# Turning and dividing the attention outputs of 8-wide heads after the last maximum, in a 12-stage kernel

## The chip, the cores and the metric

One Trainium2 chip, one core of it. The time is the device time of one execution in microseconds (us), and the figure that counts is the median of the runs. PE is the matrix engine (PEld are its weight loads, which run beside its matmuls), DVE the vector engine, ACT the scalar engine, POOL the third elementwise engine, SP the queue that issues the loads and stores. PSUM is the accumulator memory, eight banks of 128 x 512 float32; SBUF is the working memory.

## What is computed

Twelve residual stages over 2048 tokens of 128 numbers. Two of them, stage 4 and stage 10, are attention with 16 heads that are 8 wide, and only they are touched:

```
q, k, v = heads(x @ Wq + bq), heads(x @ Wk + bk), heads(x @ Wv + bv)   # 16 heads, 8 wide
# stage 10 alone: rotary turn of q and k, a bias by distance, causal mask
att = softmax(q @ k^T * scale, axis=-1)
y = att @ v                                    # 2048 x 8 for each head
x = x + y.reshape(2048, 128) @ Wo + bo
```

Stage 4 attends to all 2048 keys, stage 10 only to keys at or before the query. The other ten stages are feed-forward layers, one local attention, one linear attention and so on.

## The kernel before

Both stages are the class `Attn8`. The work is cut into 16 rounds; a round is four heads and 512 queries. A round is cut into steps of 128 keys: 16 steps a round in stage 4 (256 in all), and 4, 8, 12 or 16 in stage 10 (160 in all), where the later 512 queries see more keys. Scores are made transposed, keys on the partitions and queries along the row.

Softmax needs the maximum of each query over all keys before its scores are exponentiated. PE makes a second set of scores for this (`max`, line 1894), queries on the partitions, in whichever of banks 5, 6 and 7 is next in a ring, and DVE reduces each 128 x 512 block to one number for each query (line 2107; in stage 10 a block that touches the diagonal goes through a custom add-and-max, line 2104). These maxima run ahead of the rounds that need them. When a round's maxima are complete, DVE closes them (`close`, line 2113), POOL splits them in two parts (lines 2169, 2171), and PE turns them into a row (`max_rows`, lines 1906, 1909) that the scores take in.

The order of everything is written out by `lay_plan` as one list, and each engine runs through its own part of that list in order. In a step the list holds: up to two maxima ahead of the scores, the scores of heads 0 and 1 and of heads 2 and 3 (line 1925, banks 0 and 1, then 2 and 3), `step` (ACT takes the exponential, line 2024), further maxima, a due `max_rows`, a due `finish`, the products with v of the step before (`values`, line 1942, bank 4), further maxima. Followed through for the kernel before, the list puts 4 maxima in each of steps 0 to 235 of stage 4 and the last 2 in step 236, so 19 steps follow without any. In stage 10 the last 2 maxima stand in step 137, and 22 steps follow. In stage 10 the steps near the diagonal ("near" steps) also have a bias, which goes through ACT (2014, 2017, 2029), POOL (2177) and DVE (2120).

A round ends when its last `values` is done. ACT copies bank 4, outputs transposed with the sum of the exponentials as a ninth row of each head, to `self.OT` (line 2033, two buffers). In the second step of the next round the list has `finish`: PE turns the four 128 x 128 pieces into the next bank of the ring (line 1951), DVE takes the reciprocal of the sums (line 2127) and multiplies (line 2129) into `self.AO`, which is `g.XN`. The finish of round n stands at step 16n + 17 of stage 4, for n up to 14; the finishes of stage 10 stand at steps 5, 13, 25, 41, 57, 69, 77, 81, 85, 93, 105, 121, 137, 149 and 157. The one of round 15 follows the last step. After it PE turns all of `AO` (line 1956) and projects it (line 1963).

`self.P` holds q and k in three bfloat16 parts; SP stores them to DRAM at the start of the stage, and they are not read afterwards. `self.RC` (4 x 512 float32) is a workspace of the same opening part.

Of the kernel before, what the change touches and what calls it, by code (L numbers as in the profile page):

```python
# [8 lines left out]
ACT = mybir.ActivationFunctionType  # L9
# [1463 lines left out]
class Attn8(Stage):  # L1473
# [10 lines left out]
    def allocate(self, g):  # L1484
        ar = g.ar
        self.causal = causal = self.k == 10
        self.pre = "L3a_" if causal else "L1a_"
        self.names = ("wq", "wk", "wv", "wo", "wqr", "wkr") if causal else ("wq", "wk", "wv", "wo")
        self.scale = 8.0 ** -0.5 if causal else 0.25
        self.W = ar.f32(6 if causal else 4, 128)  # L1490
        self.bqk = ar.f32(4 if causal else 2)
        self.bvb = ar.f32(2, 128)
        if causal:
            g.wr.at = 0
            self.ROT = g.wr.f32(2, 2048)
        self.slots = slots = 2 if causal else 4
        self.RC = ar.f32(4, 512)
        self.P = ar.bf16(2, 3, 2048)
        self.rows = {name: ar.bf16(slots, 2048) for name in ("KA", "KC", "QA", "QB", "QC")}
        self.VF = ar.f32(NT * 144 + 24)  # L1500
        self.VV = self.VF[:, 0:NT * 144].rearrange("p (a b c) -> p a b c", a=NT, b=16)
        self.AO = g.XN
        self.MX = ar.f32(2, 4, 4, 4)
        self.MT = ar.f32(2, 4, 4)
        self.MN = ar.bf16(2, 4, 128)
        self.OT = ar.f32(2, 512)
        self.RD = ar.f32(2, 4, 4)
        self.junk = ar.bf16(2, 512)
        self.warm = ar.f32(2)
        if causal:  # L1510
            self.BF, self.BN = g.near_bias
            self.NB = ar.f32(2, 2, 256)
            self.F2 = ar.f32(2, 512)
        else:
            self.KEPT = ar.f32(6, 512)
            self.NQ = ar.bf16(512)
        self.PB = ar.f32(4, 1024)
        assert not causal or ar.at <= 41500 - 9216
        self.rounds = [(gr, qc) for gr in range(4) for qc in ((0, 1, 2, 3) if (gr % 2 == 0) == causal else (3, 2, 1, 0))]
        self.last_kt = [4 * qc + 3 if causal else NT - 1 for gr, qc in self.rounds]  # L1520
        self.parts = [(c, j) for c in range(4) for j in (1, 0)] if causal else [
            (0, 1), (3, 0), (1, 1), (2, 1), (3, 1), (2, 0), (0, 0), (1, 0)]
        self.lay_plan()
# [77 lines left out]
    def lay_plan(self):  # L1601
# [24 lines left out]
        finish_due = []  # L1626
        self.left[0], self.left[1] = (("xt", 2),), (("xt", 3),)
        for x in range(len(self.parts) + 2):
            if x < len(self.parts):
                c, j = self.parts[x]  # L1630
                b = 2 * (x % 2) if causal else x % 4
# [37 lines left out]
        for i, (n, kt) in enumerate(steps):  # L1669
            goal = self.target(p + area[i])  # L1670
            pairs = [self.next_max(half, goal, 3) for half in (1, 0)]
            if causal:
                order = [x[y] + (2 * x[y][1] + z,) for y in range(3) for x in pairs if y < len(x) for z in range(2)]
                slots = [[x for y, x in enumerate(order) if 4 * y // max(4, len(order)) == z] for z in range(4)]
            else:
                order = [x[y] for y in range(3) for x in pairs if y < len(x)]
                slots = [order[0:1], [], order[1:], []]
            for u in range(2):
                for x in slots[u]:
                    self.plan_max(*x)  # L1680
                self.plan.append(("score", i, n, kt, u, self.hold(2 * u, ("exp", i, 1) if u else ("left", i)) + self.hold(2 * u + 1)))
            self.plan.append(("step", i, n, kt))
            for x in slots[2]:
                self.plan_max(*x)
            if self.rows_due:
                self.plan_rows_max(self.rows_due.pop(0))
            if finish_due:
                self.plan_finish(finish_due.pop(0))
            elif side:
                self.plan_rows(side.pop(0))  # L1690
            if i >= 1:
                pn, pk = steps[i - 1]
                if pk // 4 not in self.rows_made:
                    self.plan_rows(side.pop(0))
                self.plan.append(("values", i - 1, pn, pk))
                if pk == last_kt[pn]:
                    finish_due.append(pn)
            for x in slots[3]:
                self.plan_max(*x)
            self.plan_closed()  # L1700
            p += area[i]
        self.plan.append(("values", len(steps) - 1, *steps[-1]))
        for n in finish_due + [15]:
            self.plan_finish(n)


    def wait_left(self, e, s, old):

# [140 lines left out]
    def tensor(self, e, s):  # L1849
        g, k = self.g, self.k  # L1850
        KA, KC, QA, QB, QC = (self.rows[name] for name in ("KA", "KC", "QA", "QB", "QC"))
        turn_tensor(e, s, g, k, g.XN, "xn")
        seen = set()
        for what, *x in self.plan:
            if what == "compact":
                y, c, j, b, old, old_turned = x
# [10 lines left out]
            if what == "rows":  # L1867
                i, b, old = x
                self.wait_left(e, s, old)
                for y in range(4):  # L1870
                    o = 512 * i + 128 * y
                    t = e.matmul(g.bank[b][:, 128 * y:128 * y + 128], g.XT[:, o:o + 128], self.W[:, 2, :],
                                 start=True, stop=True, skip_group_check=True)
                t.then_inc(*s.up("row", k, i))
            if what == "max":
                n, st, kc, heads = x
                (gr, qc), w = self.rounds[n], min(512, self.keys_of(n, st) - 512 * kc)
                q, i = gr % self.slots, 4 * self.rounds[n][1] + st
# [18 lines left out]
            if what == "max_rows":  # L1897
                n, b, old = x
                gr, qc = self.rounds[n]
                self.wait_left(e, s, old)  # L1900
                name = self.score_rows_in(gr, qc, False)
# [6 lines left out]
                for i in range(4):  # L1908
                    t = e.matmul(g.bank[b][:, 128 * i:128 * i + 128], self.MN[:, n % 2, i, :], g.identb[:, :], start=False,
                                 stop=True, skip_group_check=True)  # L1910
                t.then_inc(*s.up("m_turned", k, n))
            if what == "score":
                i, n, kt, u, old = x
# [5 lines left out]
                name = self.score_rows_in(gr, kt // 4, True)  # L1919
# [3 lines left out]
                for y, (K, Q) in enumerate(((KA, QA), (KA, QB), (KC, QC))):  # L1923
                    for h in (2 * u, 2 * u + 1):
                        t = e.matmul(g.bank[h][:, lo:512], K[32 * h:32 * h + 32, q, 128 * kt:128 * kt + 128],  # L1925
                                     Q[32 * h:32 * h + 32, q, queries], start=y == 0, stop=y == 2, skip_group_check=True)
                t.then_inc(*s.up("scored", k, i, u))
            if what == "values":
                i, n, kt = x
# [10 lines left out]
                for h in range(4):  # L1940
                    o = 144 * kt + 9 * (4 * gr + h)
                    t = e.matmul(g.bank[self.O][32 * h:32 * h + 32, lo:512], self.VF[:, o:o + 32],  # L1942
                                 self.PB[:, y + h // 2, 512 * (h % 2) + lo:512 * (h % 2) + 512], start=kt == 0,
                                 stop=kt == self.last_kt[n], skip_group_check=True)
                t.then_inc(*s.up("valued", k, i))
            if what == "finish":
                n, b, old = x
                self.wait_left(e, s, old)
                e.wait_ge(*s.at("ot", k, n))
                for i in range(4):  # L1950
                    t = e.transpose(g.bank[b][:, 128 * i:128 * i + 128], self.OT[:, n % 2, 128 * i:128 * i + 128], g.ident)  # L1951
                t.then_inc(*s.up("o_turned", k, n))
        for c in range(4):
            e.wait_ge(*(s.at("xt", k, c - 2, "out") if c > 1 else s.at("finished", k, 15)))
            for i in range(4):
                t = e.transpose(g.bank[c % 2][:, 128 * i:128 * i + 128], self.AO[:, 4 * c + i, :], g.ident)
            t.then_inc(*s.up("turned", k, c, "out"))
        for c in range(4):
# [3 lines left out]
            for i in range(4):  # L1962
                t = e.matmul(g.bank[2 + c % 2][:, 128 * i:128 * i + 128], g.XT[:, 512 * c + 128 * i:512 * c + 128 * i + 128],
                             self.W[:, 3, :], start=True, stop=True, skip_group_check=True)
            t.then_inc(*s.up("projected_out", k, c))

    def scalar(self, e, s):
        g, k = self.g, self.k
        turn_scalar(e, s, g, k)
        in_kept = {}  # L1970
        for what, *x in self.plan:
            if what == "first":
                y, c, j, b = x
# [8 lines left out]
            if what == "second":  # L1982
                y, c, j = x
# [4 lines left out]
            if what == "max":  # L1988
                n, st, kc, heads = x
# [8 lines left out]
            if what == "max_rows":  # L1998
                n, b, _ = x
# [4 lines left out]
            if what == "step":  # L2004
                i, n, kt = x
                near, lo = self.near_cols(n, kt), self.low(n, kt)
                for u in range(2):
                    src = g.ps[:, 1024 * u:1024 * u + 1024].rearrange("p (a b) -> p a b", a=2)
                    dst = self.PB[:, (2 * kt + u) % 4, :].rearrange("p (a b) -> p a b", a=2)
                    if u == 0 and near:  # L2010
# [3 lines left out]
                        t = e.activation(nb, src[:, :, first:end], ACT.Copy)  # L2014
# [14 lines left out]
                    e.activation(dst[:, :, first:end], nb, ACT.Exp, scale=self.scale).then_inc(*s.up("exp", k, i, 0))  # L2029
            if what == "values" and x[2] == self.last_kt[x[1]]:  # L2030
                i, n, kt = x
                e.wait_ge(*s.at("valued", k, i))
                e.activation(self.OT[:, n % 2, :], g.bank[self.O], ACT.Copy).then_inc(*s.up("ot", k, n))
        for c in range(4):
            e.wait_ge(*s.at("turned", k, c, "out"))
            e.activation(g.XT[:, chunk(c)], g.bank[c % 2], ACT.Copy).then_inc(*s.up("xt", k, c, "out"))
# [899 lines left out]
```

## Time and profile before

| | |
|---|---|
| median of 3 runs | 3428.21 us (3421.75 to 3432.43) |
| the profiled execution, its own time | 3430.28 us |
| its span, first to last instruction | 3428.5 us |
| granted TensorE clock, mean of the span | 0.929 of 2.4 GHz |
| busy share: PE, DVE, ACT, POOL | 89%, 71%, 53%, 25% |
| rounds of stage 4 | about 940 to 1600 us |
| rounds of stage 10 | about 2640 to 3165 us |

The busy shares are means over twelve stages with different limits, and matmul ends are modelled, so a PE at 98% need not be at its peak. A granted clock of 1.00 means 2.4 GHz, 0.50 means 1.2 GHz. The idle time in brackets behind an instruction is that of its engine just before it, with the instruction that ended it.

### The profile page before, as it was taken

How to read it: one execution, taken by the hardware profiler on the slowest of the kernel's cores; microseconds unless marked ns; L12 is line 12 of the kernel's file. 1: busy time of each engine (PE TensorE's matmuls, PEld its weight loads, DVE VectorE, ACT ScalarE, POOL GpSimd, SP SyncE). 2: the span in 40 equal slices, each digit the busy share in tenths (PEclk: the TensorE clock that was granted, in tenths of full speed). 3: DMA queues.
4: the chain of work that ended last, by engine and by line, in shares of the span. 5: the costliest groups of instructions: out<-in, count | busy, mean ns of one | idle time of the engine just before them, and what ended most of it. 6: DMA issues, size and time to landing. Idle time of an engine off the chain costs nothing. (4 is left out here: it accounts for less than half of the span.)

```text
span 3428.5 us, 61914 instructions
## 1 busy us (share of the span) xinstructions
PE 3045.1 (89%) x24469; PEld 1638.4 (48%) x24469; DVE 2442.0 (71%) x5485; ACT 1802.4 (53%) x3298; POOL 852.6 (25%) x809
## 2 busy tenths in 40 slices
PE   4788679998799999998899889798997998998899
PEld 3335446566322222223566657476774232333677
DVE  8898588777699999993878743645336887883533
ACT  2223347777477777776778743133222466667221
POOL 0333147865100000002967700101203111202000
PEclk9898889999699999999999989799998698899999
DMA  1065221110510000000211110002003200000100
GB/s 53 9 161 138 61 65 32 37 37 11 168 65 1 1 2 1 1 1 26 64 28 35 31 30 1 29 1 86 14 1 105 80 32 1 35 2 1 48 1 13
DMA packets 77880, 129.20 MB, mean 38 GB/s; under 512 B 12773, under 2 KB 52617, under 8 KB 77385
## 3 DMA queue, kind: packets, MB, share of 16 engines
q1 hardware_dynamic: 77592, 125.25, 12.9%
q8 instruction: 195, 3.19, 0.4%
q14 instruction: 93, 0.75, 0.1%
HBM read 77.39 MB, written 34.19 MB: 33 GB/s over the span
## 5 line engine op out<-in xcount | busy, mean ns | idle before, releaser
L2024 ACT ACTIVATE AR<-ps 128x1024 f32<-128x1024 f32 (+2 forms) x756 | 717.8, 995 | 293.1 <-PE ps L1925 223.6
L2107 DVE TENSOR_REDUCE AR<-ps 128x1 f32<-128x512 f32 x1296 | 809.3, 684 | 50.6 <-PE ps L1894 49.9
L1925 PE MATMUL ps<-AR 32*128 32x512 bf16 (+3 forms) x4992 | 538.3, 379 | 9.6 <-ACT AR L2024 5.9
L1894 PE MATMUL ps<-AR 32*128 32x512 bf16 (+3 forms) x1664 | 481.4, 400 | 42.7 <-DVE AR L2107 14.3
L1942 PE MATMUL ps<-AR 128*32 128x512 f32 (+3 forms) x3328 | 444.1, 607 | 4.4 <-ACT AR L2029 4.0
L2516 PEld LDWEIGHTS ps<-AR 128*128 128x128 f32 x3072 | 362.9, 192 | 60.4 <-issue 47.5
L2675 DVE SCALAR_TENSOR_TENSOR X<-ps,AR,X 128x128 f32<-128x128 f32 x512 | 143.7, 345 | 342.9 <-PE ps L2516 342.5
L1894 PEld LDWEIGHTS ps<-AR 32*128 32x128 bf16 x1664 | 119.6, 93 | 556.6 <-DVE AR L2107 416.8
L2516 PE MATMUL ps<-AR 128*128 128x128 f32 x3072 | 363.1, 275 | 0.0
L2491 PE MATMUL ps<-XT,AR 128*128 128x512 f32 x672 | 307.7, 594 | 0.0
L1925 PEld LDWEIGHTS ps<-AR 32*128 32x128 bf16 x4992 | 186.5, 95 | 150.2 <-ACT AR L2024 47.3
L205 POOL TENSOR_TENSOR rs<-rs,halves 128x4 f32<-128x4 f32 x48 | 49.5, 1031 | 835.2 <-DVE rs L197 835.2
L2568 ACT ACTIVATE AR<-ps,AR 128x512 f32<-128x512 f32 x144 | 98.9, 687 | 276.1 <-PE ps L2491 276.1
L1291 ACT ACTIVATE AR<-ps,AR 128x128 f32<-128x128 f32 x512 | 228.0, 469 | 15.1 <-DVE AR L1367 15.0
L2169 POOL CAST AR<-AR 128x16 bf16<-128x16 f32 x32 | 8.1, 252 | 798.8 <-DVE AR L2113 798.8
L1441 POOL TENSOR_TENSOR AR<-AR,halves 128x16 f32<-128x16 f32 x64 | 191.9, 2999 | 41.0 <-DVE AR L1360 41.0
L1437 POOL TENSOR_TENSOR AR<-AR 128x512 f32<-128x512 f32 x128 | 170.4, 1340 | 76.5 <-DVE AR L1356 76.5
L2104 DVE CUSTOM_DVE_ANT_0 AR<-ps,AR 128x512 bf16<-128x512 f32 (+3 forms) x304 | 144.3, 518 | 41.6 <-PE ps L1894 40.9
L2491 PEld LDWEIGHTS ps<-XT,AR 128*128 128x128 f32 x672 | 120.0, 190 | 109.6 <-issue 107.1
L2564 ACT ACTIVATE AR<-ps 128x512 f32<-128x512 f32 x128 | 76.4, 597 | 143.2 <-PE ps L2491 143.1
L2177 POOL TENSOR_TENSOR AR<-AR 128x512 f32<-128x512 f32 (+1 forms) x76 | 70.3, 925 | 282.0 <-ACT AR L2014 282.0
L2656 DVE TENSOR_SCALAR AR<-ps,AR 128x512 f32<-128x512 f32 x112 | 83.7, 749 | 55.0 <-PE ps L2491 55.0
(327 smaller groups left out, 5024.3 us busy)
## 6 DMA issues: line engine op xcount, KB each, us to landing
AR<-AR SPq DMA_DIRECT2D x124, 128.0 KB, 2.3
band<-AR SPq DMA_DIRECT2D x32, 450.0 KB, 5.1
AR<-band SPq DMA_DIRECT2D x32, 448.0 KB, 5.0
AR<-in_c_rot SPq DMA_DIRECT2D x64, 128.0 KB, 2.2
AR<-in_L3f_w SPq DMA_DIRECT2D x30, 256.0 KB, 5.3
rows_KA<-AR SPq DMA_DIRECT2D x32, 128.0 KB, 2.4
AR<-scr_bias SPq DMA_DIRECT2D x32, 128.0 KB, 3.2
AR<-in_L2f_w SPq DMA_DIRECT2D x30, 128.0 KB, 3.0
```

Of the source, the lines that this page charges most:

```text
L1291: t = e.activation(self.PB[:, n % 3, y, :], s8[:, y, :], ACT.Exp, scale=self.rn[:, n % 4, h:h + 1], bias=self.nb[:, n % 2, y:y + 1], accum ...
L1437: e.tensor_tensor(a, a, b, ALU.add).then_inc(*s.up("summed", k, n, j))
L1441: e.tensor_tensor(r, r, g.half[:, :], ALU.pow).then_inc(*s.up("power", k, n, "raw"))
L1894: e.matmul(g.bank[b][:, 0:w], QA[rows, q, 128 * i:128 * i + 128], KA[rows, q, 512 * first:512 * first + w], start=way != "kept", stop=True ...
L1925: t = e.matmul(g.bank[h][:, lo:512], K[32 * h:32 * h + 32, q, 128 * kt:128 * kt + 128], Q[32 * h:32 * h + 32, q, queries], start=y == 0, s ...
L1942: t = e.matmul(g.bank[self.O][32 * h:32 * h + 32, lo:512], self.VF[:, o:o + 32], self.PB[:, y + h // 2, 512 * (h % 2) + lo:512 * (h % 2) + ...
L2024: e.activation(dst[:, :, lo:512], src[:, :, lo:512], ACT.Exp, scale=self.scale).then_inc(*s.up("exp" if u else "left", k, i, *((1,) if u e ...
L2104: e.tensor_tensor_reduce(self.junk[:, h % 2, 0:w], g.bank[b][:, 0:w], self.BN[:, 4 * gr + h, z:z + w], 1.0, NEG, ALU.add, ALU.max, o).then ...
L2107: e.tensor_reduce(o, g.bank[b][:, 0:w], AXX, ALU.max).then_inc(*s.up("reduced", k, n, h, st, kc))
L2491: e.matmul(g.bank[b], self.W1[ex][:, 128 * m:128 * m + 128], g.XT[:, chunk(c)], start=True, stop=True).then_inc(*s.up("up", k, n))
L2516: t = e.matmul(g.bank[b][:, 128 * i:128 * i + 128], self.HT[:, m, 512 * c + 128 * i:512 * c + 128 * i + 128], self.W2[:, ex, m, :], start= ...
L2675: e.scalar_tensor_tensor(g.X[:, y, :], g.bank[b][:, 128 * i:128 * i + 128], self.L2[:, y, ex:ex + 1], g.X[:, y, :], ALU.mult, ALU.add).the ...
```

## The change

Each round's transposed output gets its own place in SBUF: rounds 0 to 3 in `RC`, rounds 4 to 15 in `late`, 12 x 512 float32 laid over `P`. `OT` goes. ACT waits, before it writes the first, for POOL's last subtraction that reads `RC`, and before it writes round 4's, for the eight last stores out of `P`. In `lay_plan` a due `finish` is held back until both halves of the maxima have all been put in the list; from then on one `finish` goes in each step.

```diff
@@ allocate
         self.RC = ar.f32(4, 512)
+        at = ar.at
         self.P = ar.bf16(2, 3, 2048)
+        ar.at = at
+        self.late = ar.f32(12, 512)
...
-        self.OT = ar.f32(2, 512)
@@ lay_plan
-            if finish_due:
+            if finish_due and min(self.done) == len(units):
                 self.plan_finish(finish_due.pop(0))
@@
+    def out(self, n):
+        return self.RC[:, n, :] if n < 4 else self.late[:, n - 4, :]
+
+    def wait_stored(self, e, s):
+        for c in range(8):
+            name, block = ("QA", 3) if c < 4 else ("QC", 1)
+            key = (name, block, c % 4) if self.causal else (
+                ("KA", 2, 0), ("KA", 2, 1), ("KA", 2, 2), ("KA", 2, 3), ("QA", 3, 3), ("KC", 1, 3), ("QA", 3, 2), ("QC", 1, 1))[c]
+            e.wait_ge(*s.at("d_stored%d" % c, self.k, *key))
@@ tensor, "finish"
-                    t = e.transpose(g.bank[b][:, 128 * i:128 * i + 128], self.OT[:, n % 2, 128 * i:128 * i + 128], g.ident)
+                    t = e.transpose(g.bank[b][:, 128 * i:128 * i + 128], self.out(n)[:, 128 * i:128 * i + 128], g.ident)
@@ scalar, last "values" of a round
+                if n == 0:
+                    e.wait_ge(*s.at("third", k, *self.parts[-1]))
+                if n == 4:
+                    self.wait_stored(e, s)
                 e.wait_ge(*s.at("valued", k, i))
-                e.activation(self.OT[:, n % 2, :], g.bank[self.O], ACT.Copy).then_inc(*s.up("ot", k, n))
+                e.activation(self.out(n), g.bank[self.O], ACT.Copy).then_inc(*s.up("ot", k, n))
```

## Rows read from the trace of the kernel before

**Rows 1.** Windows: stretch and length, busy us (instructions) by engine, then clock, DMA.

```profile
982.00:1523.00 541.00, 529.00 (x5101) 161.09 (x5097) 523.50 (x869) 415.82 (x442) 6.76 (x26) 1.00 0.01 1
1551.00:1594.00 43.00, 41.69 (x379) 10.45 (x375) 1.27 (x4) 35.78 (x39) 4.25 (x3) 1.00 0.01 1
2690.00:3107.00 417.00, 383.02 (x3321) 125.13 (x3317) 347.41 (x914) 269.43 (x381) 59.48 (x84) 0.88 0.04 14
3111.00:3156.00 45.00, 39.64 (x382) 10.55 (x379) 7.73 (x14) 36.76 (x58) 10.19 (x11) 0.96 0.00 1
```

**Rows 2.** Groups of instructions by shape, 982 to 1523 us: busy, mean ns, idle before.

```profile
L2107 DVE TENSOR_REDUCE AR<-ps 128x1 f32<-128x512 f32 x832 | 516.6, 683 | 15.7 <-PE ps L1894 15.6
...
L1894 PEld LDWEIGHTS ps<-AR 32*128 32x128 bf16 x830 | 57.0, 90 | 277.7 <-DVE AR L2107 275.2 <-issue 2.5
```

**Rows 3.** Timeline, stage 4: an ordinary step, and the next with a finish.

```profile
1513.38 9.94 DVE L2107 TENSOR_REDUCE AR<-ps 128x1 f32<-128x512 f32 x16 [0.83 <-PE ps L1894]
...
1517.92 0.39 PE L1894 MATMUL ps<-AR 32*128 32x512 bf16 x2
...
1520.41 0.39 PE L1894 MATMUL ps<-AR 32*128 32x512 bf16 x2
...
1522.18 0.66 PE L1951 MATMUL ps<-C,AR 128*128 128x128 f32 x4 [0.21 <-DVE AR L2107]
...
1523.23 0.25 DVE L2127 RECIPROCAL AR<-ps 128x16 f32<-128x16 f32 x1
1523.52 0.29 DVE L2129 TENSOR_TENSOR XN<-ps,AR 128x128 f32<-128x128 f32 x1
...
1523.76 0.39 PE L1894 MATMUL ps<-AR 32*128 32x512 bf16 x2
...
1524.18 6.26 DVE L2107 TENSOR_REDUCE AR<-ps 128x1 f32<-128x512 f32 x10 [0.38 <-PE ps L1894]
```

**Rows 4.** Timeline of DVE, stage 4: the finish one round earlier.

```profile
1481.54 0.25 DVE L2127 RECIPROCAL AR<-ps 128x16 f32<-128x16 f32 x1
```

**Rows 5.** Timeline, stage 4 after the last maximum: plain steps and one finish.

```profile
1558.77 1.01 PE L1925 MATMUL ps<-AR 32*128 32x512 bf16 x12
...
1560.72 1.73 PE L1925 MATMUL ps<-AR 32*128 32x512 bf16 x12
...
1562.38 0.66 PE L1951 MATMUL ps<-C,AR 128*128 128x128 f32 x4
...
1563.97 0.84 PE L1925 MATMUL ps<-AR 32*128 32x512 bf16 x12
...
1565.91 1.74 PE L1925 MATMUL ps<-AR 32*128 32x512 bf16 x12
...
1568.57 1.01 PE L1925 MATMUL ps<-AR 32*128 32x512 bf16 x12
1569.43 3.88 ACT L2024 ACTIVATE AR<-ps 128x1024 f32<-128x1024 f32 x4 [0.72 <-PE ps L1925]
```

**Rows 6.** Timeline, stage 10: a finish at the full clock.

```profile
3058.74 0.66 PE L1951 MATMUL ps<-C,AR 128*128 128x128 f32 x4
...
3059.50 0.25 DVE L2127 RECIPROCAL AR<-ps 128x16 f32<-128x16 f32 x1
3059.78 0.29 DVE L2129 TENSOR_TENSOR XN<-ps,AR 128x128 f32<-128x128 f32 x1
...
3060.75 2.48 DVE L2107 TENSOR_REDUCE AR<-ps 128x1 f32<-128x512 f32 x4 [0.68 <-PE ps L1894]
```

**Rows 7.** Timeline, stage 10: a finish at the lower clock.

```profile
2857.69 1.06 PE L1951 MATMUL ps<-C,AR 128*128 128x128 f32 x4
...
2858.69 1.94 PE L1942 MATMUL ps<-AR 128*32 128x512 f32 x8
```

**Rows 8.** Timeline, stage 10: near steps after the last maximum.

```profile
3145.17 0.66 PE L1925 MATMUL ps<-AR 32*128 32x384 bf16 x6
...
3146.69 1.07 PE L1942 MATMUL ps<-AR 128*32 128x512 f32 x8
...
3147.69 0.50 PE L1925 MATMUL ps<-AR 32*128 32x256 bf16 x6
...
3148.79 0.58 ACT L2014 ACTIVATE AR<-ps 128x512 f32<-128x512 f32 x1
```

## The prediction

> **What bounds the kernel now.** I began with the page's busy shares, which average twelve stages and say little here, and went to the windows, cut where the plan changes character. There are four such stretches [rows 1]. In the body of stage 4, where each step carries four maxima, DVE is busy 523.5 of 541 us (97%) and PE 529 (98%), at the full 2.4 GHz. In the stretch after its last maximum DVE is busy 1.3 of 43 us and PE still 97%. Stage 10 has the same two parts: DVE 83% and PE 92% at a mean clock of 0.88, then DVE 17% of 45 us.
>
> Two engines near 100% need a second view. The groups by shape show the weight loads for the maxima waiting 275 us in that stretch for DVE's reduction to release a bank, while DVE's reductions waited only 15.6 us for PE [rows 2]. So in the body PE is held by DVE. The timeline confirms it: 16 reductions take 9.94 us without a gap, 0.621 each, and one step is 1520.41 - 1517.92 = 2.49 us: four reductions [rows 3]. Whatever DVE does in the body beside reductions lengthens the stage. After the last maximum DVE has nothing to do, and the order of PE and ACT sets the step: over two steps, 1558.77 to 1563.38 without the finish, or from 1563.97 to 1568.57 = 4.60 us, so 2.30 a step, while ACT needs 3.88 for its four exponentials and idles 0.72 [rows 5]. The shorter of the two, 1563.97 to 1565.91, is 1.94: all of PE's work of a step back to back, with no wait.
>
> **What a finish costs where it stands.** In stage 4, the step with a finish is 1523.76 - 1520.41 = 3.35 us, against 2.48: 0.87 [rows 3]. The parts: reciprocal and multiply take DVE from 1523.23 to 1523.80, 0.57, and it then idles 0.38 because PE had the transposes to do and then the products with v before the next maxima. Against the whole round it holds too: 1523.23 - 1481.54 = 41.69 us [rows 3, 4], and 16 x 2.485 is 39.8, which leaves 1.9 for the finish and for the close and `max_rows` that stay. I use 0.87.
>
> **Stage 4, removed.** The finishes of rounds 0 to 13 stand in the body (steps 17 to 225, before step 236). 14 x 0.87 = 12.2 us. ACT's copy stays, and the products of the next round still wait for it. It costs nothing now, since ACT has 0.5 us free in a step whose exponentials take 1.94, and nothing in the change lengthens it.
>
> **Stage 4, added.** From step 236 on one finish a step: rounds 0 to 13 in steps 236 to 249, round 14 in step 250 instead of 241. Twenty steps are left and 15 are needed, so nothing trails behind the stage. DVE's part is hidden in its own idle time. PE's is not: four transposes, 0.59 us to the start of the products behind them (the row says 0.66, with the modelled end). A step then has 1.94 + 0.59 = 2.53 us of PE work. With the exponentials at 1.94 there is no further wait in the loop: the scores of heads 2 and 3 find their bank free, because exponentials and hand-over are done within the 2.53. So a plain step of 2.30 becomes 2.53, +0.23. The one finish shown there cost more, since it fell into the longer step of a pair: 1560.72 to 1563.97 is 3.25 against 2.66, so 0.59 [rows 5]. For step 236, which still has two maxima, I put 0.4, for step 237 with the last `max_rows` the whole 0.59, for 13 more 13 x 0.23 = 3.0, and take off the 0.59 that round 14 costs today: +3.4. Bounds: 0 if all of it disappears, 15 x 0.59 - 0.6 = 8.3 if none is absorbed. I take 3.4, because it follows from the order of PE and ACT. Stage 4: -12.2 + 3.4 = -8.8.
>
> **Stage 10, removed.** Rounds 0 to 11 (steps 5 to 121); round 12's finish at step 137 is replaced by round 0's. Here the steps are irregular. From below, a finish costs what PE spends on the transposes, 0.59. From above it is DVE's stop: 3059.50 to 3060.75 = 1.25 us between reductions [rows 6]. In five of the twelve the clock was wholly or partly at its lower level, and PE alone takes 2858.69 - 2857.69 = 1.00 [rows 7]. Some others lie at near steps where ACT and POOL have a say. The sum is between 12 x 0.59 = 7.1 and 12 x 1.25 = 15; I take stage 4's 0.87, 10.4 us, which lies near the middle of what the rows show.
>
> **Stage 10, added.** Rounds 0 to 11 move to steps 137 to 148, round 12 to 149, round 13 from 149 to 150; 14 stays at 157, so here too nothing trails. Twelve further steps get a finish. Step 138 has the last `max_rows`: 0.59. Six are plain steps (139 to 142, 148, 150): 6 x 0.23 = 1.4. Five are near steps. There PE has 1.01 us from one product's start (3146.69) to the next scores (3147.69), and ACT reads these scores only from 3148.79 on [rows 8]; most of 0.59 goes into that gap, and I put 0.15 each, 0.8. Sum 2.8, bounds 0 and 12 x 0.59 = 7.1. Stage 10: -10.4 + 2.8 = -7.6.
>
> **What costs nothing.** The wait for POOL's last subtraction and the eight waits for the stores stand in ACT's queue at the end of rounds 0 and 4. Those stores fed the loads that the first rounds read, so they ended long before; round 4 ends 80 steps in (56 in stage 10). Behind these waits stands only the copy of bank 4, covered by ACT's 0.5 us a step in stage 4. If one were late, the next round's products would wait for the copy, once. No instruction on SP or POOL and no DMA is moved. One bank of the ring is free for maxima at each round's second step; that gain is inside the 0.87.
>
> **The sum.** -8.8 - 7.6 = -16.4 us. The profiled execution took 3430.3 (span 3428.5 and 1.8 around it), so its like would take 3413.9. It lies 2.1 above the median of the runs, so I forecast 3412.
>
> **Rivals.**
> 1. *Both ends are PE's.* If the body is set by PE as much as by DVE, a finish costs there only its transposes, 0.59, and if nothing is absorbed afterwards it costs the same there: 26 x 0.59 removed, about 26 x 0.59 added, 3428. PE's 98% speaks for it; 275 us of weight loads waiting for DVE against 15.6 the other way [rows 2] speak against it for stage 4. Half of it (stage 10 alone at zero) gives 3428 - 9 = 3419. Together 0.17.
> 2. *All is hidden.* The tail takes the transposes for nothing, and stage 10 gives back 12 x 1.04 (the middle of 0.87 and 1.25 with some steps at the lower clock): -12.2 - 12.5 = -24.7, 3403. ACT's idle 0.72 in two steps speaks for it, PE's unbroken 1.94 against it. 0.10.
> 3. *The clock turns it round.* In stage 10 the clock is 0.88 where PE is 92% busy, and 1.00 in stage 4, where it is 98% [rows 1]. The change takes twelve groups of transposes out of the first. If a tenth more of those 417 us ran at the lower level (42 us, in which PE-bound work takes about twice as long), up to 21 us would be lost: -16.4 + 21 = +5, 3433. From 27 us lost on, which is 54 us more at the lower level, it is slower by over 0.3%. Against it: many of the stretches at the lower level today hold near steps with small matmuls, not places where a finish would help, and a shorter pause at DVE leaves PE denser, not thinner. 0.05, of which 0.03 slower.
> 4. *The finishes trail.* If the maxima ended so late that finishes were left for after the last step, each would cost 0.59 or more on an empty machine, 15 of them 9 us, and the gain would shrink to 7. The count of 20 and 23 steps left against 15 needed speaks against it. 0.02.
>
> The Trainium skill, "TensorE: Matmul & The Clock Gate", Part 1 (the HAM clock gate), says that the throttled clock is the default and that activity releases it. Rows 1 agree, with 0.88 against 1.00 for the less busy stretch; by that rule, PE work taken out of a sparse stretch is a risk, which is rival 3, and by the same rule the stretches that get the work are safer than before.
>
> **How the numbers follow.** The forecast's own case, between -11 and -22 us, gets 0.66; its own range is 3406 to 3417. The runs of one kernel spread over 10 us, so the median can miss its case by some 4. 0.3% is 10.3 us, about what a measurement of this kernel can tell from no change. Below 3417.9 counts as faster: nearly all of 0.66, rival 2 (0.10), which makes 0.75 with what the spread takes off. Within 0.3%: rivals 1, 4, most of the rest, 0.21. Slower: 0.04. The range runs from rival 2 to half of rival 1, 3402 to 3422.
>
> **What would show it.** Rounds of stage 4 at a distance of 41.69 - 0.87 = 40.8 us; four reductions a step with no stop except at the close; the transposes (line 1951) all after the last reduction, one group a step, steps of 2.53 us, DVE idle around its reciprocals; from last maximum to last product 3 to 4 us more than today in each stage. Wrong would be: rounds of 41 us or more, tail steps of 2.9, a body clock in stage 10 under 0.85, or ACT waiting at the end of round 4.

## The result, and the profile after

The changed kernel took 3408.50 us, median of 4 runs (3408.24 to 3412.63), against 3426.99 for the kernel before in the same comparison: ratio 0.9952, 95% interval 0.9941 to 0.9964. The forecast was 3412, in a range of 3402 to 3422. The profiled execution has a span of 3406.9 us, 21.6 less than before.

The windows of the kernel after, cut at the same places of the plan: body of stage 4, its last steps, body of stage 10, its last steps. They answer to [rows 1].

```profile
974.00:1508.00 534.00, 523.94 (x5082) 158.83 (x5092) 521.64 (x852) 419.33 (x447) 6.76 (x26) 1.00 0.01 1
1537.00:1583.00 46.00, 45.45 (x424) 15.33 (x419) 7.83 (x29) 35.71 (x38) 4.25 (x3) 1.00 0.00 1
2682.00:3082.00 400.00, 361.75 (x3264) 117.61 (x3273) 341.25 (x892) 268.96 (x381) 59.49 (x84) 0.92 0.04 15
3086.00:3133.00 47.00, 44.77 (x432) 15.46 (x424) 13.88 (x37) 37.25 (x59) 10.67 (x12) 0.94 0.01 2
```

DVE's share of the body of stage 4 rises from 97 to 98%, and in the last steps it now has work (7.8 us of 46) while PE is busy 99% of them, up from 97%.

To place the difference I use three marks that both kernels have: the first and the last close of the maxima and the last reciprocal of a stage. Stage 4 has one close, at 925.78 us before and 922.90 after, ahead of its rounds; "first close of stage 4" means the next one here, 14 rounds before the last. "Body" is from close to close, "last steps" from the last close to the last reciprocal. The timeline of DVE before (close is line 2113, reciprocal 2127), stage 4 and then stage 10:

```profile
967.76 0.22 DVE L2113 TENSOR_REDUCE AR<-AR 128x16 f32<-128x64 f32 x1
...
1551.61 0.22 DVE L2113 TENSOR_REDUCE AR<-AR 128x16 f32<-128x64 f32 x1
...
1598.92 0.26 DVE L2127 RECIPROCAL AR<-ps 128x16 f32<-128x16 f32 x1 [35.27 <-PE ps L1951]
...
2647.10 0.18 DVE L2113 TENSOR_REDUCE AR<-AR 128x16 f32<-128x16 f32 x1
...
3108.84 0.18 DVE L2113 TENSOR_REDUCE AR<-AR 128x16 f32<-128x16 f32 x1
...
3164.41 0.26 DVE L2127 RECIPROCAL AR<-ps 128x16 f32<-128x16 f32 x1 [4.21 <-PE ps L1951]
```

And after (2132 and 2146), with one more close of stage 4, the reductions behind it, and the first held finish, which stands ahead of the last close:

```profile
965.33 0.22 DVE L2132 TENSOR_REDUCE AR<-AR 128x16 f32<-128x64 f32 x1
...
1454.86 0.22 DVE L2132 TENSOR_REDUCE AR<-AR 128x16 f32<-128x64 f32 x1
...
1495.65 0.22 DVE L2132 TENSOR_REDUCE AR<-AR 128x16 f32<-128x64 f32 x1
...
1499.09 7.45 DVE L2126 TENSOR_REDUCE AR<-ps 128x1 f32<-128x512 f32 x12 [0.83 <-PE ps L1909]
...
1536.26 0.25 DVE L2146 RECIPROCAL AR<-ps 128x16 f32<-128x16 f32 x1
...
1536.93 0.22 DVE L2132 TENSOR_REDUCE AR<-AR 128x16 f32<-128x64 f32 x1
...
1588.06 0.26 DVE L2146 RECIPROCAL AR<-ps 128x16 f32<-128x16 f32 x1 [14.91 <-PE ps L1966]
...
2639.68 0.18 DVE L2132 TENSOR_REDUCE AR<-AR 128x16 f32<-128x16 f32 x1
...
3083.63 0.18 DVE L2132 TENSOR_REDUCE AR<-AR 128x16 f32<-128x16 f32 x1
...
3142.15 0.26 DVE L2146 RECIPROCAL AR<-ps 128x16 f32<-128x16 f32 x1 [4.00 <-PE ps L1966]
```

Subtracting gives the account of the 21.6 us (negative: shorter after):

| part | before | after | difference | forecast |
|---|---|---|---|---|
| start to first close of stage 4 | 967.76 | 965.33 | -2.4 | 0 |
| stage 4, body | 583.85 | 571.60 | -12.3 | -11.8 |
| stage 4, last steps | 47.31 | 51.13 | +3.8 | +3.0 |
| stages 5 to 9 | 1048.18 | 1051.62 | +3.4 | 0 |
| stage 10, body | 461.74 | 443.95 | -17.8 | -10.4 |
| stage 10, last steps | 55.57 | 58.52 | +3.0 | +2.8 |

The finish of step 236 stands ahead of the last close, so the 0.4 that the forecast put for it is counted in the body here: -12.2 + 0.4 and 3.4 - 0.4. It makes the last round of the body 1536.93 - 1495.65 = 41.28 us. What is left, +0.7, lies behind stage 10. A round of stage 4 is 1495.65 - 1454.86 = 40.79 us, where it was 41.69 [rows 3, 4]. The stretches that the change doesn't touch differ by 2 to 3 us either way, and stage 10's body by 7 more than forecast; the experiments take that up. Stages 5 to 9 took 1050.4 to 1054.0 us in the twelve profiles of the experiments, so the 1048.18 before is the odd one.

The last steps of stage 4 after, where a finish stands in every step. They answer to [rows 5]:

```profile
1559.12 0.66 PE L1966 MATMUL ps<-C,AR 128*128 128x128 f32 x4
...
1560.71 0.84 PE L1940 MATMUL ps<-AR 32*128 32x512 bf16 x12
1561.48 0.42 PEld L1966 LDWEIGHTS ps<-C,AR 128*128 128x128 f32 x4 [0.42 <-issue]
...
1562.07 1.07 PE L1957 MATMUL ps<-AR 128*32 128x512 f32 x8
...
1563.07 1.31 PE L1940 MATMUL ps<-AR 32*128 32x512 bf16 x12
1563.56 0.33 PEld L1940 LDWEIGHTS ps<-AR 32*128 32x128 bf16 x6 [0.17 <-ACT AR L2039]
...
1564.31 0.66 PE L1966 MATMUL ps<-C,AR 128*128 128x128 f32 x4
...
1565.90 0.42 PE L1940 MATMUL ps<-AR 32*128 32x512 bf16 x4
```

Two steps take 1565.90 - 1560.71 = 5.19 us, against 4.60. The short one is 2.36: twelve scores, four transposes and eight products back to back. In the long one, 2.83, the scores of heads 2 and 3 still wait for an exponential (0.17 at the weight load), and the transposes start 1.24 after the first score (1563.07 to 1564.31) where it is 0.77 in the short one (1560.71 to 1561.48). A finish costs (5.19 - 4.60) / 2 = 0.29 here.

### The profile page after: what moved, and what is told of

Same layout as the page of the kernel before. It is cut to its first block and busy times, and to the rows that moved or that the text cites. A ratio compares the mean times of both kernels' runs of the same rounds, so it can differ in the third digit from the quotient of the medians.

```text
span 3406.9 us, 61884 instructions
## 1 busy us (share of the span) xinstructions
PE 3023.7 (89%) x24429; PEld 1641.8 (48%) x24469; DVE 2440.1 (72%) x5485; ACT 1802.7 (53%) x3298; POOL 851.4 (25%) x809
```

## The experiments

All medians stand against the kernel before, run on the same chip in turn. From each profile I read the same four stretches:

| kernel | ratio (interval) | body 4 | last steps 4 | body 10 (its clock) | last steps 10 |
|---|---|---|---|---|---|
| before | | 583.85 | 47.31 | 461.74 (0.85) | 55.57 |
| after | 0.9952 (0.9941 to 0.9964) | 571.60 | 51.13 | 443.95 (0.88) | 58.52 |
| whole_again | 0.9960 (0.9944 to 0.9976) | 571.87 | 51.12 | 444.10 (0.88) | 58.48 |
| stage4_only | 0.9966 (0.9954 to 0.9977) | 571.86 | 51.13 | 451.24 (0.88) | 57.90 |
| stage10_only | 0.9988 (0.9977 to 0.9999) | 583.89 | 47.30 | 448.31 (0.87) | 55.51 |
| places_only | 0.9995 (0.9981 to 1.0009) | 583.86 | 47.31 | 455.22 (0.87) | 57.87 |
| ghost_pe | 1.0021 (1.0009 to 1.0034) | 583.80 | 51.12 | 454.70 (0.87) | 58.54 |
| ghost_dve | 0.9979 (0.9965 to 0.9992) | 575.02 | 51.11 | 445.70 (0.88) | 57.13 |
| ghost_bank4 | 0.9991 (0.9982 to 1.0000) | 579.89 | 51.13 | 447.96 (0.89) | 56.58 |
| skip_bank | 0.9968 (0.9956 to 0.9980) | 573.33 | 51.13 | 443.88 (0.88) | 58.43 |
| after_values | 0.9963 (0.9949 to 0.9977) | 572.14 | 51.28 | 444.19 (0.88) | 56.25 |
| no_finish | 0.9947 (0.9930 to 0.9964) | 571.16 | 47.11 | 451.60 (0.85) | 55.58 |
| early_after_values | 1.0006 (0.9996 to 1.0015) | 582.18 | 47.30 | 454.58 (0.88) | 57.94 |
| rows_after_values | 0.9924 (0.9911 to 0.9938) | 567.70 | 50.87 | 447.59 (0.86) | 55.99 |

Stage 4 runs at 2.4 GHz throughout, and kernels with the same plan there agree within 0.3 us. So its columns settle questions of a tenth of a microsecond per round. Stage 10 spreads by up to 10 us for one plan: `before`, `places_only` and `stage4_only` have it alike and read 461.7, 455.2 and 451.2, in the order of their clocks.

**Whole change again**, unaltered.

> The whole change once more, beside the experiments. In its first profile stage 10 shortened by 14.8 us, counted from its first close to its last finish, where the prediction had 7.6, and 34 us less of that stage ran at the lower clock. If the clock follows the change, the sum stays near -18 to -20 us in every run, and the body of stage 10 again has fewer lower-clock stretches. If that was luck of one execution, the median of the runs comes nearer to -16 us.

3412.95 us, 13.6 below the kernel before. Its profile repeats the first one's within 0.3 us in all four stretches, stage 10's body too. So it was not the profile of after that was out of line in stage 10's body, but the one of before: 461.74 at a clock of 0.85. In the medians the change is worth less here than in the first comparison, 13.6 us against 18.5.

**Each stage alone, and the places alone.**

```diff
-            if finish_due and min(self.done) == len(units):
+            if finish_due and (causal or min(self.done) == len(units)):        # stage4_only
+            if finish_due and (not causal or min(self.done) == len(units)):    # stage10_only
+            if finish_due:                                                     # places_only
```

> Places for all rounds in both stages, finishes held back in stage 4 alone. Theory (DVE's queue sets the body of stage 4): rounds of 40.8 us, stage 4 shorter by 8.4 us as in the whole change, total 8 to 9 us under the kernel before, stage 10 within its own spread. Rival (the gain is a matter of the clock in stage 10 alone): under 3 us.

3417.57 us, -9.0. Body -12.0, last steps +3.8, so -8.2: the theory's 8.4, met in the runs as well.

> Places for all rounds in both stages, finishes held back in stage 10 alone. By the prediction's terms 7.6 us less than before. If the excess of the first profile belongs to the change (fewer stretches at the lower clock once DVE no longer stops), 11 to 15 us less, and a body of stage 10 of about 400 us instead of 417. If it was chance, 6 to 9 us less in the median.

3425.14 us, -1.4, and by its interval between -0.3 and -7.9. Less than either case named. The whole change lies 4.6 below `stage4_only`, which is a second reading of the same thing. By the stretches: four profiles with the early finishes in stage 10 (`before`, `places_only`, `stage4_only`, `early_after_values`) average 455.7 in its body; six with held or no finishes there (`after`, `whole_again`, `stage10_only`, `after_values`, `skip_bank`, which also passes over a bank, and `no_finish`) average 446.0. That is 9.7, near the forecast's 10.4. At the same clock of 0.88 it is 451.2 and 454.6 against 443.9 to 444.2, 7 to 11.

The profiles flatter this, each being one execution. That of `stage10_only` was 4.3 us under the median of its runs, that of `places_only` 4.7 over. By the medians holding the finishes back in stage 10 yields 1.4 us (`stage10_only`) or 4.6 (`whole_again` under `stage4_only`), by the means of the same runs 3.1 or 3.7: about half of the 7.6 forecast. Part of it may have gone to the clock. On that chip the granted clock of the whole span averages 0.9330 over 53 executions with early finishes in stage 10 (the kernel before, `places_only`, `stage4_only`) and 0.9313 over 20 with held ones (`stage10_only`, `whole_again`). On another chip `after_values` and `skip_bank` have 0.9332, and the kernel before 0.9335. So whether the change lowers the clock stays open.

> The new places and ACT's nine new waits, but every finish where it stood before. Theory: nothing, within 3 us of the kernel before, rounds of stage 4 at 41.68 us. Rival (two buffers of outputs held something back, or a wait for a store lasts): a gain or loss of 3 us or more, and a changed time at the end of rounds 0 and 4.

3425.06 us, -1.5 with zero inside the interval; body 4 equal to the hundredth of a microsecond (583.86 against 583.85). The places and ACT's nine waits cost and bring nothing.

**What is the 0.87?** The forecast took it from the difference of two step lengths and described it as DVE's two operations and an idle 0.38. Two kernels split it, by leaving a useless copy of one engine's part at the old places of the changed kernel.

```diff
+            if finish_due and finish_due[-1] not in ghosts and min(self.done) < len(units):
+                ghosts.add(finish_due[-1])
+                self.plan_ghost(finish_due[-1])
...
+            if what == "ghost":       # ghost_pe: in tensor(), b is the next bank of the ring
+                n, b, old = x
+                self.wait_left(e, s, old)
+                e.wait_ge(*s.at("ot", k, n))
+                for i in range(4):
+                    e.transpose(g.bank[b][:, 128 * i:128 * i + 128], self.out(n)[:, 128 * i:128 * i + 128], g.ident)
...
+            if what == "ghost":       # ghost_dve: in vector()
+                y = self.ghost[:, x[0] % 2, :]
+                e.reciprocal(y[:, 128:144], self.bqk[:, 0:1].broadcast_to([128, 16]))
+                e.tensor_tensor(y[:, 0:128], self.bvb[:, 0, :], self.bvb[:, 0, :], ALU.mult)
```

> The whole change, with an unused copy of the four transposes left at each old place (bank of the ring taken, result read by nobody), so the old places keep PE's part and lose DVE's. If DVE sets the body, a round of stage 4 stays near 40.8 us (at most 41.1) and the total is within 3 us of the whole change in stage 4. If PE does, a round is 41.4 (0.59 more), 8 us in stage 4, and as much in stage 10. In stage 10 it also tells whether PE's work there changes the clock: if less PE work had raised it, the lower-clock stretches return.

3431.75 us, 7.8 above the kernel before; 3.8 of this are stage 4's last steps, which still hold the moved finishes. Body 4 is 583.80: the transposes alone, without any DVE work, bring back 12.2 of the 12.3 us. My theory fell here. The timeline of that kernel, the end of an ordinary step and then an old place:

```profile
1519.07 0.38 PE L1916 MATMUL ps<-AR 32*128 32x512 bf16 x1
1519.38 0.16 PEld L1964 LDWEIGHTS ps<-AR 128*32 128x32 f32 x8 [0.23 <-issue]
...
1521.55 0.38 PE L1916 MATMUL ps<-AR 32*128 32x512 bf16 x1
1522.14 0.42 PEld L1973 LDWEIGHTS ps<-C,AR 128*128 128x128 f32 x4 [0.51 <-DVE AR L2139]
...
1522.73 0.16 PEld L1964 LDWEIGHTS ps<-AR 128*32 128x32 f32 x8 [0.17 <-issue]
...
1524.15 4.37 DVE L2139 TENSOR_REDUCE AR<-ps 128x1 f32<-128x512 f32 x7 [0.87 <-PE ps L1916]
```

In an ordinary step the products follow the fourth maximum after 0.31 us (1519.07 to 1519.38). Here they start 1522.73 - 1521.55 = 1.18 after it: 0.87 later. Of this, 0.59 are the transposes (1522.14 to 1522.73) and 0.28 is what remains of a wait for a bank of the ring, all three of which PE had just filled. DVE stands still for exactly 0.87.

> The whole change, with a reciprocal and a multiply of the same shapes, from SBUF and waiting for nobody, left at each old place on DVE. If DVE's busy time is the cost, a round of stage 4 is longer by those 0.45 to 0.57 us, 6 to 8 us in stage 4; if DVE's wait for the transposes and the bank they took was the cost, it stays near 40.8. The prediction's 0.87 would be split into DVE's work and the rest.

3417.11 us. Body 4 is 3.3 longer than without (575.02 against 571.7), 0.24 a round. DVE's timeline at an old place:

```profile
1514.88 0.24 DVE L2150 RECIPROCAL AR<-AR 128x16 f32<-128x16 f32 x1
1515.03 0.23 DVE L2151 TENSOR_TENSOR AR<-AR 128x128 f32<-128x128 f32 x1
1515.18 3.16 DVE L2133 TENSOR_REDUCE AR<-ps 128x1 f32<-128x512 f32 x5
```

They take the 0.30 us between 1514.88 and 1515.18, with no stop behind them. (At the other old places the rounds are about 0.21 longer, 41.01 against 40.80, and one of them, 41.35, is 0.55 longer.) They are cheaper than the real pair (0.57), which reads PSUM and waits between its two instructions. DVE's part costs something only where DVE doesn't stop anyway; in the kernel before it lay inside the stop that the transposes made, and cost next to nothing more. Rounds are 41.68 with it and 41.66 without. One round of 42.02 against 41.67, 0.3 us once, recurs only in the profiles that have DVE's pair at the old places. (The equal bodies, 583.85 and 583.80, hide this: the second holds the 0.5 of the finish in step 236, the first doesn't.)

**PE's time or the ring's bank?** `ghost_bank4` puts the useless transposes in bank 4, free at that moment; `skip_bank` passes a bank over and does nothing else.

```diff
-        b = self.spare()
-        self.plan.append(("ghost", n, b, self.hold(b)))
+        self.plan.append(("ghost", n, self.O, ()))      # ghost_bank4
...
+                ghosts.add(finish_due[-1])
+                self.ring += 1                           # skip_bank
```

> As ghost_pe, but the unused transposes at the old places go to bank 4, which the copy has just emptied and the next products overwrite, so no bank of the maxima's ring is taken. The 0.87 us that ghost_pe brought back in full reads in its timeline as 0.28 of waiting for a ring bank and 0.59 of transposes. If both are real and add up, the round of stage 4 is 40.79 + 0.59 = 41.4 us. If the bank taken from the ring is the whole cost, it stays at 40.8; if PE's time is the whole cost, 41.67.

3421.58 us. Body 4 is 579.89, 8.2 above the whole change, 0.59 for each of 14. In the timeline there is no wait ahead of the transposes, and DVE's stop is their length:

```profile
1516.33 0.66 PE L1972 MATMUL ps<-C,AR 128*128 128x128 f32 x4
1516.91 1.07 PE L1963 MATMUL ps<-AR 128*32 128x512 f32 x8
...
1518.33 4.96 DVE L2138 TENSOR_REDUCE AR<-ps 128x1 f32<-128x512 f32 x8 [0.59 <-PE ps L1915]
```

> The whole change, with one bank of the ring passed over at each old place and nothing else there. If the ring, not PE's time, carries part of the cost, a round of stage 4 is 0.28 us longer (41.07), or up to 0.62 (one reduction not covered). If only PE's time counts, 40.79.

3414.20 us, body 4 573.33: 1.6 more than the whole change, 0.11 a round, less than the 0.28 named. A bank passed over with nothing behind it costs little; the 0.28 came with an instruction that stands in PE's queue ahead of the products and can't start. Why passing a bank over costs 0.11 and not nothing was not looked into. So 0.87 = 0.59 + 0.28, both PE's: its time, and its wait.

The Trainium skill, "Perfetto Trace Analysis", Identifying Performance Opportunities, says that the same gap repeating on the engine that should be saturated can mean too little PSUM for the next tile. The trace agrees for the 0.28, which went when bank 4 was used; by that rule alone the 0.59 would have gone too, and it stayed.

**How dear are the last steps?** `no_finish` leaves out the turning and dividing of rounds 0 to 14, so those parts of the output are missing.

```diff
-            if finish_due and min(self.done) == len(units):
-                self.plan_finish(finish_due.pop(0))
+            if finish_due:
+                finish_due.pop(0)
...
-        for n in finish_due + [15]:
-            self.plan_finish(n)
+        self.plan_finish(15)
```

> The whole change, but the outputs of rounds 0 to 14 are not turned and divided at all in both stages, so those parts of the output are left out; it is the floor of what moving them can bring. Body of stage 4 as in the whole change (571.7 us from first to last close), the last steps at 2.30 instead of 2.60, so from last close to last finish about 47.3 - 0.6 = 46.7 us against 51.1, and stage 10 about 2 to 3 us less in its last steps. Rival: the last steps stay long for another reason (the copy, the last max row), 50 us or more.

3408.67 us. Last steps of stage 4: 47.11 against 51.13, so the fourteen finishes that the whole change puts there cost 4.0, 0.29 each. The kernel before, with round 14's alone, has 47.31, so that one costs 0.2. The body is 571.16: 12.7 under the kernel before, and 0.4 to 0.7 under the whole change, which has the finish of step 236 in it. The body of its stage 10 ran at a clock of 0.85, so its floor for that stage can't be read from it. Its last steps there, 55.58, say nothing either: `stage10_only`, with all its finishes, has 55.51.

**Behind the products instead of ahead of them.** In `after_values` the held finishes, in `early_after_values` finishes at their old steps, in `rows_after_values` the max row's transposes (finishes held, ahead of the products as in the change):

```diff
# after_values (early_after_values has late = bool(finish_due))
-            if finish_due and min(self.done) == len(units):
-                self.plan_finish(finish_due.pop(0))
-            elif side:
+            late = finish_due and min(self.done) == len(units)
+            if side:
...
                 self.plan.append(("values", i - 1, pn, pk))
+                if late:
+                    self.plan_finish(finish_due.pop(0))
# rows_after_values
-            if self.rows_due:
-                self.plan_rows_max(self.rows_due.pop(0))
             if finish_due and min(self.done) == len(units):
...
                 if pk == last_kt[pn]:
                     finish_due.append(pn)
+            if self.rows_due:
+                self.plan_rows_max(self.rows_due.pop(0))
```

> The whole change, but in each step the finish stands behind the products with v instead of ahead of them. The work is the same, so if PE's work alone sets the last steps, they stay at 2.6 us. If the order matters (the products come 0.6 us earlier, but the next scores stay where they are), 0 to 1 us in each stage. Neither theory expects more than 2 us in total.

3411.71 us, last steps of stage 4 51.28 against 51.13. The order hardly matters there; the round with step 236, which still has maxima, is 0.4 longer (41.66 against 41.28).

> Finishes early again, one in the second step of each round as before, but behind the products instead of ahead of them; the rest as in the whole change. If the 0.28 us wait for a ring bank goes and 0.59 of transposes stays, a round of stage 4 is 41.4 us against 41.68. If DVE's two operations now stand in its way, since the transposes come when its banks are nearly empty, 41.7 or more. Neither reaches the 40.79 of the whole change.

3427.85 us. Body 4 582.18, 1.7 less than with the finishes ahead: 0.12 a round, between the two cases. The wait for the bank is gone from its timeline, but DVE's pair now stands after its last reduction and delays the next bank: the weight load of a maximum waits 0.20 us for the multiply. Far from the whole change, as expected.

> The whole change, and the max row's transposes too stand behind the products with v instead of ahead of them. In the body of stage 4 they hold PE 0.54 us and wait about 0.5 us for a bank of the ring. If that wait is the price of asking for a ring bank just after PE has filled all three, it goes when the products (1.0 us, in which DVE empties banks) come first: a round of 40.79 becomes about 40.3, 6 to 7 us less in stage 4, some less in stage 10, 3402 to 3408 in all. If only PE's 0.54 counts, nothing changes (within 2 us of the whole change).

3398.86 us, median of 5 runs, against 3424.26: the fastest here, 25 us under the kernel before, and below the whole change's interval. Body 4 is 567.70, 4.0 below the whole change, 0.29 a round, where I had named 0.5. The whole change at a `max_rows` first:

```profile
1497.12 0.10 PEld L1921 LDWEIGHTS ps<-AR,identb 128*128 128x128 bf16 x1 [0.50 <-DVE AR L2126]
...
1497.67 1.07 PE L1957 MATMUL ps<-AR 128*32 128x512 f32 x8
```

Then this kernel. The weight load no longer stands in front of the products; its wait before it falls into their 1.0 us, and DVE stops for 0.55 where it stopped for 0.83:

```profile
1494.93 1.07 PE L1957 MATMUL ps<-AR 128*32 128x512 f32 x8
1495.93 0.10 PEld L1921 LDWEIGHTS ps<-AR,identb 128*128 128x128 bf16 x1 [0.84 <-DVE AR L2126]
...
1496.90 5.66 DVE L2126 TENSOR_REDUCE AR<-ps 128x1 f32<-128x512 f32 x9 [0.55 <-PE ps L1909]
```

4 us are stage 4's. Each against its own kernel before, and on another chip, it is 11.8 better than `whole_again` (25.4 against 13.6), so some 8 are not accounted for: its one profile shows stage 10 no shorter (447.59 at 0.86), and its span, 3404.9, belongs to the slowest of the five runs.

## Why the prediction was right

**The sum.** -16.4 forecast; -18.5 in the first comparison, -13.6 in the second, with more runs. Stage 4's part, -8.8, was met (-8.4 in the first profile, -9.0 in the medians of `stage4_only`), though for a reason other than the one I gave. Stage 10's part, -7.6, was too large: -1.4 and -4.6 in the medians, -3.1 and -3.7 in the means of the same runs. That the first comparison came out beyond the forecast and not short of it is luck.

**The bound.** "In the body PE is held by DVE": right for the ordinary step, four reductions of 0.621. "Whatever DVE does in the body beside reductions lengthens the stage" was wrong as the reason for the finish. The engine at its limit stops when the engine that feeds it is late, and it was PE that was late.

**Stage 4, removed: 12.2.** Right: 12.7 by `no_finish`, 0.91 a finish, of which the held finish in step 236 takes back about 0.5. The size came from a difference of step lengths, which holds whatever its cause. The description of its parts failed: not 0.57 of DVE plus 0.38, but 0.59 of transposes plus 0.28 of waiting for a bank, shown by `ghost_pe` and `ghost_bank4`. The first rival, that both ends are PE's, was right on the mechanism and wrong on the price, since it left out the wait ahead and took nothing as absorbed behind.

**Stage 4, added: 3.4.** 4.3 measured: 3.8 in the last steps, where the forecast's terms come to 3.0, and 0.5 in step 236. The term 13 x 0.23 was too small, since a step gains 0.29. "There is no further wait in the loop" failed in every second step: 0.47 us more from its first score to the transposes. The short step is 2.36, not 2.53, since the 1.94 was not "all of PE's work of a step back to back, with no wait". Behind its products the next scores' weight load still waited for ACT. In the kernel before:

```profile
1564.74 1.07 PE L1942 MATMUL ps<-AR 128*32 128x512 f32 x8
...
1565.90 0.33 PEld L1925 LDWEIGHTS ps<-AR 32*128 32x128 bf16 x6 [1.01 <-ACT AR L2024]
```

The products take 1.17 us to the next scores there (1564.74 to 1565.91) and 1.00 after (1562.07 to 1563.07), so 0.17 was waiting: 1.94 - 0.17 + 0.59 = 2.36. The 0.59 taken off for round 14 was too much as well, since `no_finish` puts it at 0.2.

**Stage 10, removed: 10.4.** 17.8 in the pair of profiles, 9.7 as a mean over ten. The excess is the granted clock of the execution that I predicted from: 0.85 from close to close, the lowest of the plans with early finishes (0.85, 0.87, 0.88, 0.88). The 0.87 was carried over from stage 4 to steps of another kind, and the medians, with 1.4 to 4.6 us for the whole of stage 10, say that 10.4 was too much, or that the clock took part of it back. The clocks of the bodies can't tell (0.87 in the mean of either group), and one plan spreads as far as the difference.

**Stage 10, added: 2.8.** 3.0 in the pair of profiles, but by luck. 2.1 of it lies in the last four steps, into which no finish was moved, and where the clock was 0.90 before and 0.62 after:

```profile
3151.82:3164.41 12.59, 8.50 (x100) 3.20 (x96) 3.08 (x6) 8.83 (x17) 7.34 (x6) 0.90 0.00 1
```

```profile
3127.47:3142.15 14.68, 11.78 (x100) 3.82 (x96) 3.08 (x7) 8.94 (x17) 6.89 (x6) 0.62 0.00 1
```

Both kinds of plan show both cases. With the low clock at the end the last steps of stage 10 take 57.87 to 57.94 with early finishes (`places_only`, `stage4_only`, `early_after_values`) and 58.43 to 58.52 with held ones (`after`, `whole_again`, `skip_bank`); without it 55.57 (`before`) and 55.51 (`stage10_only`). So the difference is 0.6 us in the one case and nothing in the other. Those with early finishes also have a lower clock in the middle (0.94 and 0.89 in steps 144 to 151 of `before`, 1.00 in the same steps of `after`), so what the moved finishes cost at an even clock isn't shown. Plain steps cost 0.29 as in stage 4, near steps nothing instead of 0.15. Scores after, from the first of the near steps 144 to 147, with a finish in each, to the step behind them; then the same for the near steps 152 to 155 of the kernel before, of the same shape and without a finish:

```profile
3099.33 1.38 PE L1940 MATMUL ps<-AR 32*128 32x512 bf16 x12
...
3108.35 0.84 PE L1940 MATMUL ps<-AR 32*128 32x512 bf16 x12
```

```profile
3142.77 1.48 PE L1925 MATMUL ps<-AR 32*128 32x512 bf16 x12
...
3151.82 0.84 PE L1925 MATMUL ps<-AR 32*128 32x512 bf16 x12
```

9.02 us with four finishes, 9.05 without. In the kernel before, steps 144 to 147 themselves took 9.76 at a clock of 0.94.

**What costs nothing.** Right, by `places_only`. ACT writes round 4's copy at 1139.18 us without a wait ahead of it:

```profile
1139.18 0.60 ACT L2052 ACTIVATE AR<-ps 128x512 f32<-128x512 f32 x1
```

**The rivals.** All hidden: no, 4.0 in stage 4. The clock turning it round: not as a whole, since both comparisons of the change are faster; but the clock of the whole span, 0.9313 against 0.9330 on one chip, leaves room for a small part of it. Body 10 doesn't show it: 0.87 with the transposes kept (`ghost_pe`), 0.88 without them. For stage 10 the medians (1.4 and 4.6) lie between the zero of the first rival's half and the forecast's 7.6. Finishes that trail: none, the last one stands alone behind the stage as before.

**The signs named.** Rounds of 40.8 us: 40.79. Steps of 2.53: 2.60. Last steps 3 to 4 us longer in each stage: 3.8 in stage 4; in stage 10 3.0, of which 2.1 go with the clock at the end.

## What to carry to other kernels

When one engine works without a gap and another fills a small ring of banks for it, the dear thing is whatever delays the filler, not only what the busy engine does itself: 0.59 us of transposes cost 0.87 there, and two vector operations beside them next to nothing. Move such work behind the busy stretch, where it cost 0.29 in stage 4, and put anything else that asks for a bank of the ring behind a long instruction that uses none, not right behind the one that filled the last bank. A cost read as a difference of two step lengths was safe to forecast with in the stage where it was read, and not in another one; its split among engines needs a kernel that keeps one part and drops the other. Where the clock changes within a stretch, a pair of profiles can't price the change, and the medians of many runs must.

## What the runs showed of the hardware that I had not expected

The granted clock of one and the same plan varies between executions (0.85, 0.87, 0.88 over the body of stage 10), and with it that stretch by 10 us of 455, more than the change was worth there by the medians; stage 4, at 1.00 throughout, repeated within 0.3 us. A low clock in the last four steps of stage 10 came and went with one and the same plan, and cost 2 to 3 us. Useless float32 transposes of four 128 x 128 blocks hold PE for 0.59 us at 2.4 GHz, and their full length passes to a vector engine that is 98% busy.
